# A fused cross-attention kernel: the mask moves from TensorE products to ScalarE copies into the banks of scores

## The chip, the cores and the metric

The kernel runs on one core of one Trainium2 chip. The metric is the device time of one execution in microseconds (us), from the first to the last instruction and what lies around them. Lower is better.

## The reference, cut to what matters

The input is 32 sequences of 64 tokens with 128 features, a context of the same shape, and a mask of 32 x 64 booleans that says for each sequence which keys are valid. Three attention layers follow one another, each with 16 heads of 64: self-attention with a causal mask, cross-attention and a feed-forward network (128, 512, 128), and a third attention with rotary positions.

```python
scores = jnp.einsum('bhqd,bhkd->bhqk', q, k)
if causal:
    scores = jnp.where(causal_mask[None, None], NEG_INF, scores)
if padding_mask is not None:
    scores = jnp.where(padding_mask[:, None, None, :], scores, NEG_INF)
attn = jax.nn.softmax(scores / math.sqrt(DK), axis=-1)
out = jnp.einsum('bhqk,bhkd->bhqd', attn, v)
```

After each layer comes a residual sum and a layer norm. The kernel adds -1e30 to a masked score instead of replacing it.

## The kernel before, in words

**Units.** A unit is two sequences (128 tokens) in one layer. There are 16 units a layer, N = 48 in all, and one loop over steps `u` from FIRST = -2 to N + 1 that every engine walks in its own program order; only semaphores tie the engines together. In step `u` the kernel computes scores and softmax of unit `u`, turns and weights the probabilities of unit `u - 1` and `u - 2`, and projects queries (even `u`) or keys (odd `u`) of a later pair of units.

**Banks.** PSUM has eight banks of 128 x 512 f32. Two hold scores (`ps_s`), two the weighted values (`ps_o`), and four (`ps_p`) form a ring for everything else. `fills(u)` (line 59) is the list of what TensorE puts into the ring in step `u`, in order: T (tokens turned), V0 and V1 (values), P0 and P1 (probabilities turned), Q0 to Q3 or K0 to K3 (queries or keys; Qa, Qb, Ka, Kb in the rotary layer), Y (output projection), FT, F1, F2 (feed-forward). A fill waits until the fill four places earlier has been emptied by its engine (line 418 ff.). So in an odd step K0 waits for the copy of V0 out of its bank, and K1 for that of V1; in an even step, where T comes first, Q0 waits for V0 and Q1 for V1.

**TensorE in a step** (lines 521 to 535): `scores(u)`, then `weight_values(u)` (line 400), then the fills. `scores` (line 370) waits until VectorE has read the scores of the unit before (`shifted`), then issues four products with a 64 x 64 identity (line 388) that write the mask of each sequence into the four quarters of the two score banks, 512 columns each with the 64 keys repeated over 8 heads. Then 64 products of one head each (line 395) add to them.

**ScalarE in a step** (lines 597 to 618): it copies the two `ps_o` banks out (line 568), then walks the fills it has to empty. Ahead of each of the first two of them that isn't T it puts one exponential (`exponentials`, line 571, over 128 x 512). The order in an odd step is: heads, heads, exp 0, copy V0, exp 1, copy V1, copy P0, copy P1, copies of K0, K2, K3. In an even step T stands ahead of exp 0. In a step with feed-forward the order is exp 0, V0, exp 1, FT, V1, P0, P1. VectorE empties K1 or Q1, and all of the rotary Qa to Kb.

**VectorE in a step** (`vector_order`, line 126): two maxima over the score banks (line 698), two subtractions from them (line 702, they release `shifted`), T or FT's low part, the sum of the exponentials (line 709, after exp 1), reciprocal, emptying, two scalings (line 721), emptying, and the layer norm's statistics.

**The mask table.** The SP queue loads `mask_u8` (line 326), all 16 x 2 x 64 bytes on each of 128 partitions. VectorE makes from it the bf16 table `mask` (lines 744 to 751) for units 0 to 3 in step -1 and for the rest in step 2, and `valid` (lines 753 to 761, a maximum over the keys) in steps 0, 3 and 5. Products of `eye` with itself into `ps_s[0]` (line 514, `keep_clock`) run in the first microseconds.

**Steps with extra work.** Steps 14, 15, 16 and 30, 31, 32 split the weights of the next layer on ScalarE and VectorE (`split_high`, `split_rest`). In steps 16 and 32 V0 and V1 stand at the end of the fills. Steps 21 to 35, odd, have the feed-forward. Steps 30 to 45 project with rotary tables; steps 46 and on project nothing.

Of the kernel before, what the change touches and what calls it, by code (L numbers as in the profile page):

```python
# [6 lines left out]
ALU = mybir.AluOpType  # L7
# [90 lines left out]
ALL_FILLS = [(u, n, j, who) for u in range(FIRST, END) for n, j, who in fills(u)]  # L98

SCORED = Tally(lambda u: [()] if attends(u) else [])  # L100
SHIFTED = Tally(lambda u: [(0,), (1,)] if attends(u) else [])
# [36 lines left out]
def build(nc, a, out):  # L138
    ctx = ExitStack()
    with ctx:  # L140
# [40 lines left out]

        mask_u8 = sb("mask_u8", [128, UNITS, 2, S], mybir.dt.uint8)
        mask = sb("mask", [128, 2, UNITS, 2, S], BF16)
        causal = sb("causal", [128, S], BF16)
# [68 lines left out]
        act_emptied = sem("act_emptied")  # L253
        dve_emptied = sem("dve_emptied")
        scored = sem("scored")
        shifted = sem("shifted")
# [24 lines left out]
        READY = 4  # L281
        FIRST_MASKED, FIRST_VALID, MASKED, VALID, OTHER_VALID = 2, 5, 7, 10, 13

# [32 lines left out]
        def _(sp):  # L316
# [8 lines left out]
            sp.dma_start(columns[:, :], a["columns"]).then_inc(first_loaded, 16)  # L325
            sp.dma_start(mask_u8[:, :, :, :], a["mask_BxS2_bf1"].rearrange("(u b) k -> u b k", b=2).partition_broadcast(128))\
              .then_inc(mask_loaded, 16)
            sp.dma_start(w_raw[2][:, :], weight(0, "v")).then_inc(w_loaded[2], 16)
# [33 lines left out]
        def _(pe):  # L362
# [7 lines left out]
            def scores(u):  # L370
                par, v, layer = u // 2 % 2, u % 2, u // UNITS

                if SHIFTED.before(u):
                    pe.wait_ge(shifted, SHIFTED.before(u))

# [7 lines left out]

                for h in range(2):
                    for b in range(2):
                        of = slice(64 * h, 64 * h + 64)
                        m = mask[of, 0 if layer == 0 else 1, u % UNITS, b:b + 1, :]
                        mm(ps_s[h ^ b][64 * b:64 * b + 64, :], eye_bf[of, of], m.broadcast_to([64, 8, S]),  # L388
                           start=True, stop=False, skip_group_check=True)
                for p in range(PAIRS):  # L390
# [122 lines left out]

            def keep_clock(n):

                for _ in range(n):
                    mm(ps_s[0][:, 0:128], eye[:, :], eye[:, :], start=True, stop=True)

            pe.wait_ge(setup_pool, EYES)
            keep_clock(2)  # L520
            for u in range(FIRST, END):
                if u in (0, READY):
                    pe.wait_ge(setup_dve, MASKED if u else FIRST_MASKED)
                if attends(u):
                    scores(u)
                if u == 2:
                    pe.wait_ge(bvwo_read, 2)
                if finishes(u):
                    weight_values(u)
                for at, (name, j, _) in enumerate(fills(u)):  # L530
                    fill(u, at, name, j)
                    if u == FIRST and name == "T":
                        keep_clock(4)
                if u == 1:
                    bias_of_values()

        @block.scalar
        def _(act):
# [32 lines left out]
            def exponentials(u, j):  # L571
                act.wait_ge(shifted, SHIFTED.at(u, j))
                p = probs[:, u % 2, j::2, :]
                nc.scalar.activation(p, p, ACT.Exp, scale=float(D) ** -0.5).then_inc(exped, 1)  # L574

            def split_high(u, after_input=False):
# [20 lines left out]
            for u in range(FIRST, END):  # L597
# [7 lines left out]
                for at, (name, j, who) in enumerate(fills(u)):  # L605
                    if "A" not in who:
                        continue
                    if waiting and name not in ("O", "T"):
                        exponentials(u, waiting.pop(0))
                    empty(u, at, name, j)  # L610
                    if name == "T":
                        if u == FIRST:
                            split_high(u)
                        split_high(u, after_input=True)
                        if u == -2:
                            act.wait_ge(first_loaded, 16)
# [4 lines left out]
        def _(dve):  # L621
# [122 lines left out]
            def masks(units, count):  # L744
                V.tensor_scalar(mask[:, 1, units, :, :], mask_u8[:, units, :, :], -NEG, NEG, ALU.mult, ALU.add)\
                 .then_inc(setup_dve, 1)
                dve.wait_ge(setup_dve, count - 1)
                n = units.stop - units.start
                V.tensor_tensor(mask[:, 0, units, :, :].rearrange("q u b k -> q (u b) k"),
                                mask[:, 1, units, :, :].rearrange("q u b k -> q (u b) k"),  # L750
                                causal[:, None, :].broadcast_to([128, 2 * n, S]), ALU.min).then_inc(setup_dve, 1)

            def keys_at_all(kind, units, masked, count):

                dve.wait_ge(setup_dve, masked)
                for b in range(2):
                    of = slice(64 * b, 64 * b + 64)
                    V.tensor_reduce(valid[of, kind, units], mask[of, kind, units, b, :], AX_X, ALU.max).then_inc(setup_dve, 1)
                dve.wait_ge(setup_dve, count - 1)
# [3 lines left out]
            def before_m1():  # L763
                dve.wait_ge(mask_loaded, 16)
                dve.wait_ge(setup_pool, CAUSAL)
# [212 lines left out]
```

## Time and profile before

| what | value |
|---|---|
| times of three runs | 607.12 us median, 605.61 to 608.26 |
| the profiled execution | 603.87 us, span 602.1 us |
| granted TensorE clock, mean | 0.99 |
| TensorE products, weight loads | 555.6 us (92%), 509.2 us (85%) |
| VectorE, ScalarE, GpSimd | 459.0 us (76%), 302.1 us (50%), 335.5 us (56%) |
| mask products (line 388) | 192, 19.7 us busy in all |
| exponentials (line 574) | 96, mean 638 ns |

Matmuls overlap each other, so a busy TensorE is not one at its peak; the spacing of starts says more than durations do. In the timeline a row of several instructions has the start of the first and the length of all of them. "idle before <-releaser" names how long the engine had stood still and what ended that.

### The profile page before, as it was taken

The page shows a single profiled execution, that of the slowest core. Times are in us where ns is not written, and L with a number is a line of the kernel's source. Part 1 is how long each engine was busy: PE and PEld are TensorE (multiplying, and loading weights), DVE is VectorE, ACT ScalarE, POOL GpSimd, SP SyncE. Part 2 cuts the span into 40 slices and gives each one's busy share as a digit, 9 for nine tenths or more (in the row PEclk, how much of TensorE's full clock was granted, in tenths as well). Part 3 has the DMA queues.
Part 4 walks back from the last instruction along what each step waited for, and adds up shares of the span by engine and source line. Part 5 has one row for each costly group of instructions (what it writes and reads, how often), then busy time and mean ns, then how long its engine had stood idle before and what let it go on. Part 6 is the DMA issues. An engine that isn't in the chain of part 4 may idle for free.

```text
span 602.1 us, 22151 instructions
## 1 busy us (share of the span) xinstructions
PE 555.6 (92%) x9632; PEld 509.2 (85%) x9632; DVE 459.0 (76%) x902; ACT 302.1 (50%) x647; POOL 335.5 (56%) x665
## 2 busy tenths in 40 slices
PE   6699999999998999999999988899999989999984
PEld 6588798989897988988989878789898979898874
DVE  4977877777777767677767798888888878888862
ACT  6365666575866666557565742242322424222252
POOL 1613535354436353648457496877676555465635
PEclk9979999999999999999999998999999999999999
DMA  8900000000111100000000000000000000000000
GB/s 244 282 2 3 3 2 2 2 4 2 37 37 37 38 4 2 3 2 3 2 3 3 2 3 1 1 3 2 7 7 7 7 10 7 7 7 7 5 12 14
DMA packets 10975, 12.44 MB, mean 21 GB/s; under 512 B 1024, under 2 KB 8704, under 8 KB 10880
## 3 DMA queue, kind: packets, MB, share of 16 engines
q1 hardware_dynamic: 10880, 11.04, 6.2%
q8 instruction: 76, 1.25, 0.9%
q14 instruction: 19, 0.16, 0.1%
HBM read 9.99 MB, written 1.05 MB: 18 GB/s over the span
## 4 chain that ended last, share of the span: by engine, by line
PE 60%; DVE 19%; ACT 8%; POOL 8%; issue 4%; DMA 1%; SPq 0%; POOLq 0%; ACTq 0%; DVEq 0%
PE ps_p L366 10%; PE ps_p L481 10%; PE ps_p L367 8%; PE ps_p L368 8%; PE ps_s L395 5%; PE ps_o L410 5%; PE ps_p L455 3%; ACT probs L574 3%; DVE top L698 3%; DVE probs L721 3%; PE ps_p L503 2%; ACT vv L549 2%; DVE rope_b L655 2%; ACT headsT L568 2%; PE ps_s L388 2%
## 5 line engine op out<-in xcount | busy, mean ns | idle before, releaser
L568 ACT ACTIVATE headsT<-ps_o 128x512 f32<-128x512 f32 x96 | 52.2, 596 | 206.9 <-PE ps_o L410 206.9
L481 PE MATMUL ps_p<-wo,headsT 128*128 128x128 f32 x768 | 94.1, 276 | 2.3 <-ACT headsT L568 1.3
L481 PEld LDWEIGHTS ps_p<-wo,headsT 128*128 128x128 f32 x768 | 89.7, 192 | 3.6 <-DVE rope_a L655 1.5
L709 DVE TENSOR_REDUCE total<-probs 128x16 f32<-128x1024 f32 x48 | 58.4, 1216 | 36.2 <-ACT probs L574 36.2
L698 DVE TENSOR_REDUCE top<-ps_s 128x8 f32<-128x512 f32 x96 | 61.7, 685 | 26.3 <-PE ps_s L395 26.1
L847 POOL TENSOR_TENSOR small<-mv,epsilon 128x1 f32<-128x1 f32 x48 | 17.9, 374 | 113.0 <-DVE mv L691 111.8
L721 DVE TENSOR_TENSOR probs<-probs,rinv 128x512 f32<-128x512 f32 x96 | 68.2, 713 | 0.0
L574 ACT ACTIVATE probs<-probs 128x512 f32<-128x512 f32 x96 | 61.2, 638 | 12.7 <-DVE probs L702 12.7
L366 PE MATMUL ps_p<-xT_hi,wq_hi 128*128 128x256 f32 x192 | 59.5, 310 | 5.9 <-DVE xT_lo L642 3.3
L455 PE MATMUL ps_p<-eye,probs 128*128 128x128 f32 x384 | 53.9, 275 | 9.7 <-ACT vv L549 2.9
L549 ACT ACTIVATE vv<-ps_p 128x512 f32<-128x512 f32 x96 | 57.5, 599 | 9.3 <-PE ps_p L450 9.1
L455 PEld LDWEIGHTS ps_p<-eye,probs 128*128 128x128 f32 x384 | 44.2, 140 | 20.8 <-issue 6.2
L702 DVE TENSOR_TENSOR probs<-ps_s,top 128x512 f32<-128x512 f32 x96 | 61.3, 680 | 0.0
L827 POOL TENSOR_TENSOR qT<-rope_a,rope_b 128x512 f32<-128x512 f32 x32 | 45.7, 1440 | 26.2 <-DVE rope_b L655 25.2
L395 PEld LDWEIGHTS ps_s<-kT,qT 64*64 64x64 f32 x3072 | 53.2, 135 | 3.3
L410 PE MATMUL ps_o<-probsT,vv 64*64 64x64 f32 x3072 | 53.8, 218 | 2.3 <-issue 2.3
L551 ACT ACTIVATE probsT<-ps_p 128x512 f32<-128x512 f32 x96 | 53.5, 618 | 1.7 <-PE ps_p L455 1.6
L367 PE MATMUL ps_p<-xT_lo,wq_hi 128*128 128x256 f32 x192 | 54.3, 283 | 0.0
L368 PE MATMUL ps_p<-xT_hi,wq_lo 128*128 128x256 f32 x192 | 54.1, 282 | 0.0
L557 ACT ACTIVATE qT<-ps_p,columns 128x256 f32<-128x256 f32 x96 | 39.0, 489 | 28.7 <-PE ps_p L368 28.6
L395 PE MATMUL ps_s<-kT,qT 64*64 64x64 f32 x3072 | 53.0, 218 | 0.0
L410 PEld LDWEIGHTS ps_o<-probsT,vv 64*64 64x64 f32 x3072 | 49.5, 135 | 2.8 <-issue 2.5
(144 smaller groups left out, 1480.3 us busy)
## 6 DMA issues: line engine op xcount, KB each, us to landing
out<-y_out SPq DMA_DIRECT2D x16, 64.0 KB, 1.5
X<-in_x SPq DMA_DIRECT2D x1, 768.0 KB, 8.0
across<-in_across SPq DMA_DIRECT2D x1, 704.0 KB, 10.4
wq_raw<-in_L_xattn_sa_wq SPq DMA_DIRECT2D x2, 256.0 KB, 3.1
wk_raw<-in_L_xattn_sa_wk SPq DMA_DIRECT2D x1, 512.0 KB, 5.1
wv_raw<-in_L_xattn_sa_wv SPq DMA_DIRECT2D x1, 512.0 KB, 7.7
wo<-in_L_xattn_sa_wo SPq DMA_DIRECT2D x1, 512.0 KB, 8.8
wo<-in_L_xattn_ca_wo SPq DMA_DIRECT2D x1, 512.0 KB, 10.1
```

Of the source, the lines that this page charges most:

```text
L366: mm(dst, w[0], x[0], start=True, stop=False)
L367: mm(dst, w[0], x[1], start=False, stop=False)
L368: return mm(dst, w[1], x[0], start=False, stop=True)
L395: last = mm(ps_s[h ^ b][64 * b:64 * b + 64, 64 * p:64 * p + 64], qT[of, par, p, t:t + S], kT[of, par, p, t:t + S], start=False, stop=True, ...
L410: last = mm(ps_o[b][64 * c:64 * c + 64, 64 * p:64 * p + 64], vv[of, w % 2, c, p, :], probsT[of, p // HALF, q:q + 64], start=True, stop=Tru ...
L455: last = nc.tensor.transpose(bank[:, 128 * pp:128 * pp + 128], probs[:, (u - 1) % 2, at_head:at_head + 2, :].rearrange("q h k -> q (h k)") ...
L481: last = mm(bank[:, 0:E], headsT[:, p, :, :].rearrange("r b q -> r (b q)"), wo[:, layer % 2, p, :], start=(p == 0), stop=(p == PAIRS - 1))
L549: ins = nc.scalar.activation(vv[:, u % 2, j, :, :].rearrange("k p d -> k (p d)"), bank[:, :], ACT.Copy)
L568: nc.scalar.activation(headsT[:, :, b, :], ps_o[b][:, :].rearrange("r (p q) -> r p q", q=S), ACT.Copy)\
L574: nc.scalar.activation(p, p, ACT.Exp, scale=float(D) ** -0.5).then_inc(exped, 1)
L698: V.tensor_reduce(top[:, j, :], score_heads(j), AX_X, ALU.max).then_inc(dve_step, 1)
L721: V.tensor_tensor(p, p, rinv[:, 8 * j:8 * j + 8, None].broadcast_to([128, 8, S]), ALU.mult)\
```

## The change

The mask products leave TensorE. ScalarE writes the masks: after exponential `j` of unit `u` it copies the mask of unit `u + 1` from SBUF into score bank `j`, and TensorE's score products add to what lies there. The table is now by query: partitions 0 to 63 hold the masks of the unit's first sequence, 64 to 127 those of the second, so it has half as many columns; it is loaded by two DMAs instead of one. `open_scores` takes the place of `keep_clock`: four products into each score bank at the start.

```diff
-        mask_u8 = sb("mask_u8", [128, UNITS, 2, S], mybir.dt.uint8)
-        mask = sb("mask", [128, 2, UNITS, 2, S], BF16)
+        mask_u8 = sb("mask_u8", [128, UNITS, S], mybir.dt.uint8)
+        mask = sb("mask", [128, 2, UNITS, S], BF16)
...
-            sp.dma_start(mask_u8[:, :, :, :], a["mask_BxS2_bf1"].rearrange("(u b) k -> u b k", b=2).partition_broadcast(128))\
-              .then_inc(mask_loaded, 16)
+            for b in range(2):
+                rows_of = a["mask_BxS2_bf1"].rearrange("(u b) k -> b u k", b=2)[b, :, :]
+                sp.dma_start(mask_u8[64 * b:64 * b + 64, :, :], rows_of.partition_broadcast(64)).then_inc(mask_loaded, 16)
...
             def scores(u):
...
-                if SHIFTED.before(u):
-                    pe.wait_ge(shifted, SHIFTED.before(u))
+                pe.wait_ge(masked, OPENED.at(u, 1))
...
-                for h in range(2):
-                    for b in range(2):
-                        of = slice(64 * h, 64 * h + 64)
-                        m = mask[of, 0 if layer == 0 else 1, u % UNITS, b:b + 1, :]
-                        mm(ps_s[h ^ b][64 * b:64 * b + 64, :], eye_bf[of, of], m.broadcast_to([64, 8, S]),
-                           start=True, stop=False, skip_group_check=True)
...
-            def keep_clock(n):
-
-                for _ in range(n):
-                    mm(ps_s[0][:, 0:128], eye[:, :], eye[:, :], start=True, stop=True)
+            def open_scores(j):
+
+
+                for k in range(4):
+                    last = mm(ps_s[j][:, 128 * k:128 * k + 128], eye[:, :], eye[:, :], start=(k == 0), stop=(k == 3),
+                              skip_group_check=True)
+                last.then_inc(opened, 1)
 
             pe.wait_ge(setup_pool, EYES)
-            keep_clock(2)
+            open_scores(0)
             for u in range(FIRST, END):
-                if u in (0, READY):
-                    pe.wait_ge(setup_dve, MASKED if u else FIRST_MASKED)
                 if attends(u):
                     scores(u)
...
                     if u == FIRST and name == "T":
-                        keep_clock(4)
+                        open_scores(1)
...
                 nc.scalar.activation(p, p, ACT.Exp, scale=float(D) ** -0.5).then_inc(exped, 1)
+                if attends(u + 1):
+                    put_masks(u + 1, j)
+
+            def put_masks(u, j):
+
+                if u == 0:
+                    act.wait_ge(opened, j + 1)
+                else:
+                    act.wait_ge(shifted, SHIFTED.at(u - 1, j))
+                if u in (0, READY):
+                    act.wait_ge(setup_dve, MASKED if u else FIRST_MASKED)
+                m = mask[:, u // UNITS and 1, u % UNITS, None, :].broadcast_to([128, PAIRS, S])
+                nc.scalar.activation(ps_s[j][:, :].rearrange("q (p k) -> q p k", k=S), m, ACT.Copy).then_inc(masked, 1)
...
                     empty(u, at, name, j)
+                    if (u, name, j) == (-1, "K", 0):
+                        for k in range(2):
+                            put_masks(0, k)
...
-                V.tensor_scalar(mask[:, 1, units, :, :], mask_u8[:, units, :, :], -NEG, NEG, ALU.mult, ALU.add)\
-                 .then_inc(setup_dve, 1)
+                V.tensor_scalar(mask[:, 1, units, :], mask_u8[:, units, :], -NEG, NEG, ALU.mult, ALU.add).then_inc(setup_dve, 1)
...
-                for b in range(2):
-                    of = slice(64 * b, 64 * b + 64)
-                    V.tensor_reduce(valid[of, kind, units], mask[of, kind, units, b, :], AX_X, ALU.max).then_inc(setup_dve, 1)
+                V.tensor_reduce(valid[:, kind, units], mask[:, kind, units, :], AX_X, ALU.max).then_inc(setup_dve, 1)
...
-                dve.wait_ge(mask_loaded, 16)
+                dve.wait_ge(mask_loaded, 32)
```
The constants FIRST_MASKED, FIRST_VALID, MASKED, VALID, OTHER_VALID go from 2, 5, 7, 10, 13 to 2, 4, 6, 8, 10, as `keys_at_all` has one reduction instead of two.

## Rows read from the trace of the kernel before

**Rows 1.** Groups of instructions, each form apart: the mask products of TensorE

```profile
L388 PE MATMUL ps_s<-mask,eye_bf 64*64 64x512 bf16 x192 | 19.7, 399 | 5.3 <-DVE kT L313 3.1 <-issue 2.1
```

**Rows 2.** Waits, TensorE's weight loads: total us, times, longest us

```profile
PEld ps_p L366 <- ACT vv L549: 17.5, 36, 2.5
```

**Rows 3.** Timeline of TensorE, 104 to 115 us: steps 8 (even) and 9 (odd)

```profile
104.75 0.39 PE L366 MATMUL ps_p<-xT_hi,wq_hi 128*128 128x256 f32 x1
...
108.87 0.41 PE L388 MATMUL ps_s<-mask,eye_bf 64*64 64x512 bf16 x4
109.11 1.10 PE L395 MATMUL ps_s<-kT,qT 64*64 64x64 f32 x64
...
113.38 0.38 PE L366 MATMUL ps_p<-xT_hi,wk_hi 128*128 128x256 f32 x1
...
114.39 0.39 PE L366 MATMUL ps_p<-xT_hi,wk_hi 128*128 128x256 f32 x1
```

**Rows 4.** Timeline of ScalarE over the same two steps

```profile
104.08 0.62 ACT L549 ACTIVATE vv<-ps_p 128x512 f32<-128x512 f32 x1
...
112.21 0.63 ACT L574 ACTIVATE probs<-probs 128x512 f32<-128x512 f32 x1
112.75 0.58 ACT L549 ACTIVATE vv<-ps_p 128x512 f32<-128x512 f32 x1
113.22 0.62 ACT L574 ACTIVATE probs<-probs 128x512 f32<-128x512 f32 x1
113.74 0.59 ACT L549 ACTIVATE vv<-ps_p 128x512 f32<-128x512 f32 x1
```

**Rows 5.** Timeline of VectorE, 110 to 115 us: step 9

```profile
110.29 1.29 DVE L698 TENSOR_REDUCE top<-ps_s 128x8 f32<-128x512 f32 x2 [1.33 <-PE ps_s L395]
111.50 1.28 DVE L702 TENSOR_TENSOR probs<-ps_s,top 128x512 f32<-128x512 f32 x2
```

**Rows 6.** Timeline of three engines, 259 to 261 us: a step with feed-forward

```profile
259.70 0.37 ACT L547 ACTIVATE x2T_hi<-ps_p 128x256 fp32r<-128x256 f32 x1
...
260.10 0.42 DVE L645 TENSOR_TENSOR x2T_lo<-ps_p,x2T_hi 128x256 fp32r<-128x256 f32 x1 [1.38 <-ACT x2T_hi L547]
...
260.63 0.35 PE L366 MATMUL ps_p<-cT_hi,wk_hi 128*128 128x256 f32 x1 [0.64 <-ACT vv L549]
```

**Rows 7.** Timeline of VectorE and TensorE, 510 to 519 us: step 41, odd and rotary

```profile
510.17 1.22 DVE L709 TENSOR_REDUCE total<-probs 128x16 f32<-128x1024 f32 x1 [1.11 <-ACT probs L574]
...
518.88 0.41 PE L388 MATMUL ps_s<-mask,eye_bf 64*64 64x512 bf16 x4 [0.63 <-DVE kT L313]
```

**Rows 8.** Timeline of the start: ScalarE and TensorE ahead of unit 0's scores

```profile
11.36 1.06 ACT L591 ACTIVATE wv_hi<-wv_raw 128x1024 fp32r<-128x1024 f32 x1 [0.82 <-DMA wv_raw<-in_L_xattn_sa_wv]
12.32 2.28 ACT L557 ACTIVATE kT<-ps_p,columns 128x256 f32<-128x256 f32 x6
...
14.70 0.41 PE L388 MATMUL ps_s<-mask,eye_bf 64*64 64x512 bf16 x4 [1.83 <-issue]
```

**Rows 9.** DMA view of 5.6 to 6.0 us (mostly 208-byte rows): packets and share

```profile
DMA packets 99, 0.06 MB, mean 139 GB/s; under 512 B 88, under 2 KB 88, under 8 KB 99
...
q1 hardware_dynamic: 99, 0.06, 54.7%
```

**Rows 10.** DMA view of 6.4 to 6.8 us (the mask's 2-KB rows)

```profile
DMA packets 26, 0.07 MB, mean 179 GB/s; under 512 B 1, under 2 KB 1, under 8 KB 26
...
q1 hardware_dynamic: 26, 0.07, 136.9%
```

**Rows 11.** Groups of instructions, each form apart: VectorE's maxima over the mask table

```profile
L758 DVE TENSOR_REDUCE valid<-mask 64x16 f32<-64x1024 bf16 x2 | 2.4, 1210 | 0.0
L758 DVE TENSOR_REDUCE valid<-mask 64x12 f32<-64x768 bf16 x2 | 1.9, 942 | 0.0
```

**Rows 12.** TensorE after a long stall; busy time in 30 to 37 us (after POOL the clock)

```profile
31.23 0.58 PE L366 MATMUL ps_p<-xT_hi,wk_hi 128*128 128x256 f32 x1 [2.22 <-ACT vv L549]
...
30.00:37.00 7.00, 5.77 (x27) 5.77 (x28) 5.14 (x10) 4.91 (x11) 1.25 (x1) 0.52 0.00 0
```

More of the change, by code:

```diff
@@ L98 @@
 ALL_FILLS = [(u, n, j, who) for u in range(FIRST, END) for n, j, who in fills(u)]
+OPENED = Tally(lambda u: [(0,), (1,)] if attends(u) else [])
 SCORED = Tally(lambda u: [()] if attends(u) else [])
@@ L254, in build @@
         dve_emptied = sem("dve_emptied")
+        opened = sem("opened")
+        masked = sem("masked")
         scored = sem("scored")
@@ L281, in build @@
         READY = 4
-        FIRST_MASKED, FIRST_VALID, MASKED, VALID, OTHER_VALID = 2, 5, 7, 10, 13
+        FIRST_MASKED, FIRST_VALID, MASKED, VALID, OTHER_VALID = 2, 4, 6, 8, 10
         def parts_ready(layer, n):
@@ L744, in masks @@
             def masks(units, count):
-                V.tensor_scalar(mask[:, 1, units, :, :], mask_u8[:, units, :, :], -NEG, NEG, ALU.mult, ALU.add)\
-                 .then_inc(setup_dve, 1)
+                V.tensor_scalar(mask[:, 1, units, :], mask_u8[:, units, :], -NEG, NEG, ALU.mult, ALU.add).then_inc(setup_dve, 1)
                 dve.wait_ge(setup_dve, count - 1)
                 n = units.stop - units.start
-                V.tensor_tensor(mask[:, 0, units, :, :].rearrange("q u b k -> q (u b) k"),
-                                mask[:, 1, units, :, :].rearrange("q u b k -> q (u b) k"),
-                                causal[:, None, :].broadcast_to([128, 2 * n, S]), ALU.min).then_inc(setup_dve, 1)
+                V.tensor_tensor(mask[:, 0, units, :], mask[:, 1, units, :], causal[:, None, :].broadcast_to([128, n, S]),
+                                ALU.min).then_inc(setup_dve, 1)
             def keys_at_all(kind, units, masked, count):
                 dve.wait_ge(setup_dve, masked)
-                for b in range(2):
-                    of = slice(64 * b, 64 * b + 64)
-                    V.tensor_reduce(valid[of, kind, units], mask[of, kind, units, b, :], AX_X, ALU.max).then_inc(setup_dve, 1)
+                V.tensor_reduce(valid[:, kind, units], mask[:, kind, units, :], AX_X, ALU.max).then_inc(setup_dve, 1)
                 dve.wait_ge(setup_dve, count - 1)
```

## The prediction

> **What bounds the kernel now.** I read the groups by form first, then the waits, then the timeline of one quiet pair of steps (8 and 9), where the order of every instruction can be seen. The mask products look cheap: 192 of them, but only 19.7 us busy in all, since the four of a unit run side by side [rows 1]. The waits say that TensorE's weight loads stood still 36 times for ScalarE's copy of values, 17.5 us in all [rows 2]. The timeline shows why. K0 starts at 113.38 and K1 at 114.39 [rows 3]; the copies of V0 and V1 out of the same banks end at 112.75 + 0.58 = 113.33 and 113.74 + 0.59 = 114.33 [rows 4]. TensorE starts 0.05 us after each. The even step is the same: Q1 starts at 104.75 [rows 3], V1's copy ends at 104.08 + 0.62 = 104.70 [rows 4]. So from the scores to the second projection a step is a chain: scores, two maxima and a subtraction on VectorE [rows 5], exp 0, V0's copy, exp 1, V1's copy, K1 or Q1. ScalarE's share of 50% doesn't matter there; its order does. After K1 TensorE runs on without a stop to the next scores.
>
> **The change, part by part.** A quiet step first.
>
> Mask products removed: the four start at 108.87 and the score products at 109.11 [rows 3]. That is 0.24 us a unit, at the head of the chain: VectorE's maximum waits for the scores' end [rows 5], so exp 0 comes 0.24 us earlier. In an even step the maximum is late for VectorE's own reasons, but there exp 0 stands behind heads and T on ScalarE, which follow TensorE and move up too.
>
> Mask copies added: ScalarE has one 128 x 512 copy more behind each exponential, ahead of V0's and V1's. No such write into a score bank is in the trace. What one takes on a full engine is the spacing of starts: 0.54 us (112.21 to 112.75) and 0.52 us (113.22 to 113.74) behind an exponential, which reads SBUF as the mask copy does, and 0.47 us (112.75 to 113.22) behind a copy out of PSUM [rows 4]. The bounds are 0.47 and 0.54; I take 0.52. V0 is then emptied 0.52 us later and V1 1.04 us. K0 starts 0.52 us later; it takes 0.72 us without stalls, so K1, held by V1, starts 1.04 us later. Both waits are already binding, so nothing absorbs it: what follows (P0 and P1 copied 1.04 us later) is needed 0.7 us and more after K1 and is no new wait. A quiet step grows by 1.04 - 0.24 = 0.80 us. ScalarE makes up for it in its idle time ahead of the next heads, but TensorE doesn't get it back.
>
> One rule of the Trainium skill bears on the price: ScalarE: Activation LUTs, section Step-by-step, says that PSUM is the lower-latency destination for an ACTIVATE. No run here has a ScalarE write into PSUM. By it each copy might take the lower bound, and the sum would come out some 3.5 us lower.
>
> With feed-forward, the order is exp 0, V0, exp 1, FT, V1. K0 needs FT's low part: ScalarE at 259.70, VectorE at 260.10 + 0.42 = 260.52, K0 at 260.63 [rows 6]. FT now stands behind both mask copies, so K0 starts 1.04 us later: again 0.80 us net.
>
> Steps where it is so: 1 to 13, 15, 17 to 29, 33 and 35, and the even ones from 34 to 44, whose projections TensorE bounds; 13 + 1 + 13 + 2 + 6 = 35 steps, 35 x 0.80 = 28.0 us.
>
> Odd rotary steps without feed-forward (37, 39, 41, 43, 45): VectorE works from the sum at 510.17 without a pause to the last key sum, for which TensorE waits 0.63 us at 518.88 [rows 7]. The sum waits for exp 1 alone, which has one mask copy ahead of it: 0.52 - 0.24 = 0.28 us, 5 x 0.28 = 1.4 us.
>
> Steps 14, 16, 30, 31, 32: splitting weights on VectorE holds the low parts longer than ScalarE is late, or V0 and V1 stand last. Only the removed products count: -5 x 0.24 = -1.2 us. Step 46 has no projection, but Y takes V0's bank: +0.3 us. Step 47 has no mask behind it: about 0.
>
> Start: the two mask copies of unit 0 stand on ScalarE between the copies of K0 and K2; that run goes from 12.32 to 14.60 and releases the scores at 14.70 [rows 8]. +1.04 - 0.24 = 0.8 us. The mask's load stands in the SP queue ahead of that of the V weights, and ScalarE waits for those at 11.36 [rows 8], so each us of the mask's load is a us of the start. Before, it is 128 packets of 2 KB, 8 on each DMA engine; 26 packets, nearly all such, took 136.9% of 16 engines in 0.4 us: 8.76 us / 26 = 337 ns each [rows 10], 2.7 us an engine. After, a partition's row is 16 pieces of 64 bytes from places 128 bytes apart, so 2048 packets, 128 an engine. The nearest packets are those of 208 bytes: 99 with 54.7% of 16 engines in 0.4 us are 35 ns each, and some 25 ns if the 11 large ones are taken out [rows 9]. 128 x 25 ns = 3.2 us, 0.5 us more than now; with the second issue I take +0.7 us. Bounds: -2.7 us (packets for nothing) and 128 x 337 ns - 2.7 = +40 us (each as dear as the mask's rows now). I keep near the small packets, but the same few bytes are read by 64 partitions, which may be what makes the 2-KB rows dear; so +8 us belongs in the range. The Trainium skill, DMA: Bandwidth & Descriptors, Specifications, speaks against this edit: below 512 bytes a transfer isn't at line rate and becomes a read-modify-write. It gives no price; with packets twice as dear as rows 9 show, the start would take 3 us more.
>
> Half the table on VectorE: the conversions in step 2 are hidden behind TensorE. The maxima over the table in steps 3 and 5 were late work ahead of the scores' maxima: 1.9 us and 2.4 us become half [rows 11], -0.95 - 1.2 = -2.15 us. The products that open the banks are covered by the wait for the first weights; if that cover were gone, two more products cost under 1 us.
>
> Sum: 28.0 + 1.4 - 1.2 + 0.3 + 0.8 + 0.7 - 2.15 = +27.9 us. Against the profiled execution's own 603.87 us that makes 631.7; that execution is 3.2 us below the median of the runs, 607.12. Against the median it is **635.0 us**, 4.6% slower, which I forecast.
>
> **The rivals.**
>
> 1. Faster: TensorE is the bound and ScalarE's slack swallows the copies. Then only removals count: 48 x 0.24 + 2.15 = -13.7 us, 593.4. For it: TensorE 92% busy, ScalarE 50%. It needs the copies to fall behind the copy of V1, or to take under 0.12 us each (two of them against 0.24). Against it: the 36 waits [rows 2] and the 0.05 us between copy and product at both places. 4%.
> 2. Partly hidden: K1's delay is won back within the step, because waits for later banks or for VectorE vanish, so that only exp 1's delay counts everywhere, as in step 41. 47 x 0.28 + 0.8 + 0.7 - 2.15 = +12.5 us, 619.6. For it: VectorE is 76% busy and shares the chain. Against it: TensorE has no later stop in steps 8 and 9. 9%.
> 3. A dear load: small packets at 80 to 337 ns. +7 to +40 us on top, 642 to 675. For it: the rows of one place [rows 10]. Against it: rows 9. 6%.
> 4. The clock: TensorE stood still for 2.22 us until 31.23, the last of several stops, and the granted clock was 0.52 over 30 to 37 us [rows 12], so that it ran mostly at 1.2 GHz instead of 2.4; 7 us did the work of 3.6. If the longer stalls bring three to five such stretches, 10 to 17 us are added: 645 to 652. Against it: the new stalls are about 1 us, and stalls of that length left the mean granted clock at 0.99 over the whole execution. 5%.
> 5. It doesn't do what it says, for instance ScalarE's writes wait for something else than `shifted`: nothing in the diff shows it, and the times would be those of 2 or 3.
>
> **How the numbers follow.** Forecast 76%, the rivals 4, 9, 6 and 5%. The forecast's own bounds are 625 (copies at 0.47 us, cheap packets, the profiled execution's level) and 644 (0.54 us, +8 us of load). The range takes in rival 2 and the near end of 3 and 4: 619 to 648. A measurement of this kernel tells about 0.5% (3 us) from no change. Faster by more than that: rival 1, 0.04. Within it: the low tail of rival 2, 0.03. Slower: 0.93.
>
> **What would show it.** In the profile after: mask copies of about 0.6 us, 96 of them, starting 0.5 us after each exponential; V1's copy 1.5 us behind V0's instead of 1.0; K1 or Q1 still 0.05 us after V1's copy; TensorE's waits for that copy longer by about 0.5 us each; a pair of quiet steps 1.6 us longer; scores of unit 0 at about 16.2 us. The forecast is wrong if the second projection starts well after V1's copy, if a pair of steps is no longer than before, or if the V weights land several us later.

## The result

| | before | after |
|---|---|---|
| median, us | 606.57 (605.61 to 608.26, 4 runs) | 628.75 (628.05 to 636.12, 4 runs) |
| profiled execution, us | 603.87 | 628.05 |
| its span, us | 602.1 | 626.3 |
| mean granted clock | 0.990 | 0.987 |

The changed kernel is slower: the ratio is 1.040, with a 95% interval of 1.036 to 1.044. By the medians it takes 22.2 us more, by the profiled executions 24.2 us; 27.9 us were forecast.

The page of the kernel after, parts 1 and 4 (busy time of each engine; the chain that ended last, by engine), and two of its groups of instructions (out <- in, busy us, mean ns):

```profile
PE 554.9 (89%) x9444; PEld 505.7 (81%) x9444; DVE 455.7 (73%) x899; ACT 350.9 (56%) x743; POOL 337.1 (54%) x665
...
PE 52%; ACT 30%; DVE 12%; issue 3%; POOL 2%; DMA 1%; SPq 1%; ACTq 0%; POOLq 0%; DVEq 0%
...
L392 PE MATMUL ps_s<-kT,qT 64*64 64x64 f32 x3072 | 56.1, 222 | 5.9 <-DVE kT L316 3.0
...
L585 ACT ACTIVATE ps_s<-mask 128x512 f32<-128x512 bf16 x96 | 57.7, 602 | 0.0
```

The waits of the kernel after, for the first instruction of a projection, held by the copy of values (total us, times, longest us):

```profile
PEld ps_p L370 <- ACT vv L547: 53.4, 73, 3.0
PE ps_p L370 <- ACT vv L547: 35.8, 61, 2.7
```

ScalarE is still busy for only 56% of the span, yet its share of the chain went from 8% to 30%. The wait of [rows 2] went from 17.5 us in 36 places to 53.4 us in 73. Where a wait of 36 became one of 73, K0 or Q0, behind V0's copy, has joined K1 or Q1.

The same quiet step 9 as in [rows 3], TensorE's timeline of the kernel after:

```profile
110.02 1.16 PE L392 MATMUL ps_s<-kT,qT 64*64 64x64 f32 x64
...
114.86 0.39 PE L370 MATMUL ps_p<-xT_hi,wk_hi 128*128 128x256 f32 x1 [0.28 <-ACT vv L547]
...
116.39 0.38 PE L370 MATMUL ps_p<-xT_hi,wk_hi 128*128 128x256 f32 x1 [0.55 <-ACT vv L547]
```

and ScalarE's, which answers to [rows 4]:

```profile
113.17 0.63 ACT L572 ACTIVATE probs<-probs 128x512 f32<-128x512 f32 x1
113.71 0.58 ACT L585 ACTIVATE ps_s<-mask 128x512 f32<-128x512 bf16 x1
114.23 0.58 ACT L547 ACTIVATE vv<-ps_p 128x512 f32<-128x512 f32 x1
114.71 0.62 ACT L572 ACTIVATE probs<-probs 128x512 f32<-128x512 f32 x1
115.23 0.59 ACT L585 ACTIVATE ps_s<-mask 128x512 f32<-128x512 bf16 x1
115.75 0.58 ACT L547 ACTIVATE vv<-ps_p 128x512 f32<-128x512 f32 x1
```

V0's copy ends at 114.23 + 0.58 = 114.81 and K0 starts at 114.86; V1's ends at 116.33 and K1 starts at 116.39. Each mask copy takes ScalarE 0.52 us (113.71 to 114.23, and 115.23 to 115.75), and each copy of values stands later by just that.

**Where the 24.2 us came.** The growth of every step is read from the start of each unit's first product into the score banks (a mask product before, a score product after). Those of units 0 and 47 are 565.04 us apart before and 588.76 after. Grouped as the prediction grouped them:

| | forecast, us | measured, us |
|---|---|---|
| ahead of unit 0's first product, and step 0 | +0.8 (copies) + 0.7 (load) | +0.46 (ahead) + 0.17 (step 0) |
| 27 quiet steps apart from the next two rows | 27 x 0.80 = 21.6 | +22.94 (0.85 on average) |
| steps 21, 23, 25, 27, 29 (odd, feed-forward) | 5 x 0.80 = 4.0 | +2.28 |
| steps 1, 3, 5 | 3 x 0.80 - 2.15 = +0.25 | -3.25 + 0.02 - 0.51 = -3.74 |
| odd rotary 37, 39, 41, 43, 45 | +1.4 | +1.74 |
| steps 14, 16, 30, 31, 32 | -1.2 | +1.44 |
| step 46 | +0.3 | -1.11 |
| sum | +27.9 | +24.18 |

Of the 27 quiet steps 24 grew by 0.84 to 1.01 us. Step 15 grew by 0.44, and steps 40 and 42 by -0.53 and +2.52, as a pause of TensorE moved from the one to the other (below).

### The profile page after: what moved, and what is told of

It is laid out like the page before. It is cut to its first block, busy times and chain, and to the rows that moved or that the text cites. A ratio compares the mean times of both kernels' runs of the same rounds, so it can differ in the third digit from the quotient of the medians.

```text
span 626.3 us, 21872 instructions
## 1 busy us (share of the span) xinstructions
PE 554.9 (89%) x9444; PEld 505.7 (81%) x9444; DVE 455.7 (73%) x899; ACT 350.9 (56%) x743; POOL 337.1 (54%) x665
## 4 chain that ended last, share of the span: by engine, by line
PE 52%; ACT 30%; DVE 12%; issue 3%; POOL 2%; DMA 1%; SPq 1%; ACTq 0%; POOLq 0%; DVEq 0%
PE ps_p L478 11%; PE ps_p L370 9%; PE ps_s L392 8%; ACT probs L572 8%; ACT headsT L566 7%; PE ps_p L371 7%; PE ps_p L372 7%; ACT vv L547 7%; PE ps_o L407 7%; ACT ps_s L585 7%; PE ps_p L500 2%; DVE rope_a L669 2%; DVE probs L735 2%; DVE total L723 2%; DVE rope_b L669 1%
## 5 line engine op out<-in xcount | busy, mean ns | idle before, releaser
L735 DVE TENSOR_TENSOR probs<-probs,rinv 128x512 f32<-128x512 f32 x96 | 65.4, 685 | 0.0
L392 PE MATMUL ps_s<-kT,qT 64*64 64x64 f32 x3072 | 56.1, 222 | 5.9 <-DVE kT L316 3.0
L392 PEld LDWEIGHTS ps_s<-kT,qT 64*64 64x64 f32 x3072 | 49.6, 135 | 12.8 <-issue 7.8
L585 ACT ACTIVATE ps_s<-mask 128x512 f32<-128x512 bf16 x96 | 57.7, 602 | 0.0
L370 PEld LDWEIGHTS ps_p<-xT_hi,wq_hi 128*128 128x128 f32 x192 | 36.7, 191 | 22.0 <-ACT vv L547 16.1
```

The lines of the kernel that those rows point to most:

```text
L370: mm(dst, w[0], x[0], start=True, stop=False)
L392: last = mm(ps_s[h ^ b][64 * b:64 * b + 64, 64 * p:64 * p + 64], qT[of, par, p, t:t + S], kT[of, par, p, t:t + S], start=False, stop=True, ...
L585: nc.scalar.activation(ps_s[j][:, :].rearrange("q (p k) -> q p k", k=S), m, ACT.Copy).then_inc(masked, 1)
L735: V.tensor_tensor(p, p, rinv[:, 8 * j:8 * j + 8, None].broadcast_to([128, 8, S]), ALU.mult)\
```

## The experiments

Theory: the price is the two mask copies' place in ScalarE's sequence, ahead of V0's and V1's copies, 0.52 us each; TensorE's removed products give back some 0.2 us. Rivals: the work itself costs it wherever it stands; the load in small packets costs or gains; TensorE's score products are slower for adding to ScalarE's data. The comparisons below are each with the kernel before, run beside it.

**e1_late_gap.** Both mask copies of a step in ScalarE's idle time: behind the copy of Q0 in an even step, K3 in an odd one, F1 with feed-forward, P1 in the rotary layer.

```diff
-                if attends(u + 1):
-                    put_masks(u + 1, j)
...
+                    if attends(u) and attends(u + 1) and (name, j) == mask_place(u):
+                        for k in LATE:
+                            put_masks(u + 1, k)
```

> The changed kernel, but ScalarE writes both masks later in the step: behind the copy of Q0 (even steps), of K3 (odd steps), of F1's first half (steps with feed-forward), or of P1 (rotary steps). Theory A (the cost is the place, two writes ahead of V1's copy; work on ScalarE as such is free): V0's and V1's copies are back where they were, about 8 us below the kernel before (near 598 us): 3 us from the start, 0.2 us a step from the removed products, less 0.2 to 0.4 us in the ten odd steps where ScalarE has no gap left. Theory B (the added work or TensorE's adding to a written bank costs in itself): 606 us or more.

Measured: 594.83 us (593.6 to 596.53), ratio 0.982 (0.978 to 0.985). The same 96 copies, and the kernel is faster than both. ScalarE's timeline of e1, step 9:

```profile
106.86 0.63 ACT L583 ACTIVATE probs<-probs 128x512 f32<-128x512 f32 x1
107.40 0.58 ACT L558 ACTIVATE vv<-ps_p 128x512 f32<-128x512 f32 x1
107.87 0.62 ACT L583 ACTIVATE probs<-probs 128x512 f32<-128x512 f32 x1
108.39 0.59 ACT L558 ACTIVATE vv<-ps_p 128x512 f32<-128x512 f32 x1
108.87 1.09 ACT L560 ACTIVATE probsT<-ps_p 128x512 f32<-128x512 f32 x2
109.82 2.51 ACT L566 ACTIVATE kT<-ps_p,columns 128x256 f32<-128x256 f32 x6
112.21 1.13 ACT L594 ACTIVATE ps_s<-mask 128x512 f32<-128x512 bf16 x2
```

and TensorE's:

```profile
109.04 0.39 PE L381 MATMUL ps_p<-xT_hi,wk_hi 128*128 128x256 f32 x1
...
113.40 0.81 PE L403 MATMUL ps_s<-kT,qT 64*64 64x64 f32 x40 [0.16 <-ACT ps_s L594]
```

Exponentials and copies of values stand as close as in [rows 4], and the wait for the copy of values is back at 15.3 us in 36 places. Even steps are 0.17 to 0.20 us shorter than before, odd ones 0.04 longer, since there the next scores wait 0.16 us for the mask copy that ends at 113.34. That is what was expected. The profiled execution, 596.43 us, is 7.4 us below that of the kernel before, where about 8 were expected; most of the other executions were shorter (the median is 10 us below that of the kernel before), and no trace shows what differed in them.

**e2_late_p1.** The same with both copies behind P1's in every step but step 0.

```diff
+def mask_place(u):
+    return ("P", 1) if u else ("Q", 0)
```

> Both masks behind the copy of P1 in every step. Theory A: nearly as fast as the version in the gaps, about 600 to 603 us, as K0's copy is late for Y's bank by 0.4 us in odd steps. Theory B: as above, 606 us or more.

Measured: 597.76 us (596.13 to 598.52), ratio 0.986 (0.983 to 0.989). Even steps are 0.18 to 0.20 us shorter than before, but odd ones grow by 0.41, as there the masks stand ahead of the copies of K. The time is 2 us under the 600 to 603 expected. The place within ScalarE's later work is worth 3 us, against e1; the place ahead of V0's and V1's copies costs 31 us, against e2.

**e3_bank1_late.** Only bank 1's mask behind P1; bank 0's stays behind exponential 0.

```diff
-LATE = (0, 1)
+LATE = (1,)
```

> Only the mask of bank 1 behind P1's copy, that of bank 0 still ahead of V0's. Theory A: V1's copy is late by one write (0.52 us) instead of two, so a quiet step grows by 0.52 - 0.19 = 0.33 us instead of 0.85: about 615 us, some 13 us below the changed kernel. Theory B: within 3 us of the changed kernel.

Measured: 612.0 us (611.27 to 613.56), ratio 1.009 (1.006 to 1.013). A quiet step grows by 0.33 to 0.41 us. Two early copies, one, none: +0.85, +0.33 and -0.18 us for an even step, so a copy costs 0.52 us whether it is the first or the second, and nothing when it is late. That holds for even steps. An odd step grows by 0.41 in e3 and in e2 alike: there the copies behind P1 already cost 0.6 us (-0.19 without any, in e5), and one early copy adds nothing to it. The whole came out 3 us under the 615 expected.

**e4_write_beside.** The kernel before with the change's mask copies added at the change's places; the mask products stay, wait for the copies (`masked`, in place of `shifted`) and overwrite them.

```diff
+                if attends(u + 1):
...
+                    m = mask[:, (u + 1) // UNITS and 1, (u + 1) % UNITS, 0:1, :].broadcast_to([128, PAIRS, S])
+                    nc.scalar.activation(ps_s[j][:, :].rearrange("q (p k) -> q p k", k=S), m, ACT.Copy).then_inc(masked, 1)
```

> The kernel before with its mask products kept, and ScalarE's writes added at the changed kernel's places (TensorE then overwrites them). This is the added cost alone, without the removal and without the start's changes. Theory A: quiet steps grow by 1.04 us, in all 33 to 37 us: about 641 us, slower than the changed kernel by 12. If the start's changes gave nothing (rival): about 637 us.

Measured: 649.07 us (647.11 to 650.4), ratio 1.071 (1.066 to 1.075): +44 us by the medians. A quiet step grows by 1.04 us, 2 x 0.52 to the hundredth, the 27 of them by 28.1 us. TensorE's timeline of e4, step 10, shows the same two stops as the kernel after:

```profile
123.12 0.39 PE L367 MATMUL ps_p<-xT_hi,wk_hi 128*128 128x256 f32 x1 [0.27 <-ACT vv L550]
...
124.65 0.39 PE L367 MATMUL ps_p<-xT_hi,wk_hi 128*128 128x256 f32 x1 [0.55 <-ACT vv L550]
```

Most of the 8 us above the 641 expected lie in a few steps that grew by 1.5 to 2.7 us (5, 21, 29, 30, 40), some 6 us more in all than their like. Busy time by windows of e4 (the number before the last two is the granted clock; the columns are the window, its length, and PE, PEld, DVE, ACT, POOL busy):

```profile
80.00:84.00 4.00, 3.84 (x23) 3.57 (x22) 2.59 (x6) 2.92 (x8) 0.00 (x0) 0.66 0.00 0
84.00:88.00 4.00, 4.00 (x150) 3.74 (x148) 2.27 (x6) 0.82 (x3) 1.26 (x4) 1.00 0.01 4
...
255.00:260.00 5.00, 3.84 (x19) 3.48 (x18) 2.43 (x5) 3.28 (x8) 0.00 (x0) 0.68 0.01 3
```

Each of the two stands behind a wait of TensorE for the copy of values that the longer step made longer:

```profile
78.91 0.38 PE L367 MATMUL ps_p<-xT_hi,wk_hi 128*128 128x256 f32 x1 [1.86 <-ACT vv L550]
...
256.55 0.36 PE L367 MATMUL ps_p<-cT_hi,wk_hi 128*128 128x256 f32 x1 [1.16 <-ACT vv L550]
```

In windows of 10 us the mean clock is under 0.95 in nine of e4's, against three of the kernel before and five of the kernel after. TensorE ran part of such a stretch at 1.2 instead of 2.4 GHz, and each stretch costs 1 to 1.7 us. So the forecast's fourth rival exists, and the stops ahead of these two stretches were of 1.9 and 1.2 us. A stop of that length doesn't settle it: the same one of 1.16 us ends at 284.3, 310.3 and 336.3 in e4, and in the five odd steps with feed-forward of the changed kernel, with the clock at full behind it, while in e6 (below) two of these five are followed by a slow stretch. In the changed kernel, whose steps are 0.2 us shorter, such a stretch lengthened step 30 against the kernel before; those in step 1 are told below.

**e5_no_products.** The kernel before without the mask products, nothing in their place: the masks aren't applied. The price of the removal alone.

```diff
-                        mm(ps_s[h ^ b][64 * b:64 * b + 64, :], eye_bf[of, of], m.broadcast_to([64, 8, S]),
-                           start=True, stop=False, skip_group_check=True)
...
-                                      start=False, stop=True, skip_group_check=True)
+                                      start=True, stop=True, skip_group_check=True)
```

> The kernel before without its mask products: no mask is applied at all, so this is the removal alone. If a unit's four products cost what the start of the scores moves (0.24 us): 11.5 us less, 595 us. If they cost what quiet steps of the changed kernel show (1.04 - 0.85 = 0.19 us): 9 us less, 597.5 us. If VectorE or GpSimd absorb half of it: 601 us or more.

Measured: 599.37 us (598.43 to 602.36), ratio 0.989 (0.985 to 0.994): -6.7 us by the medians, between the 9 us expected at 0.19 a step and the 5 or less of the last theory. A quiet step is 0.18 to 0.20 us shorter, not 0.24. TensorE's timeline of e5:

```profile
108.63 1.16 PE L389 MATMUL ps_s<-kT,qT 64*64 64x64 f32 x64
```

The score products now take 1.16 us instead of the 1.10 of [rows 3], whether ScalarE's data lies in the bank (after) or not (e5). So adding to ScalarE's data costs nothing. Perhaps the mask products used to cover the start of the first ones; that was not tried. In the steps with feed-forward a pair of steps gains nothing (-0.19 and +0.18): the pair isn't bound by the chain of [rows 3] there. And 1.04 - 0.19 = 0.85 us is the changed kernel's quiet step: the two halves add up.

**e6_row_load.** The change with the old load of the mask (one DMA, whole rows of 2 KB on all partitions); the table is halved when VectorE converts it.

```diff
-            for b in range(2):
-                rows_of = a["mask_BxS2_bf1"].rearrange("(u b) k -> b u k", b=2)[b, :, :]
-                sp.dma_start(mask_u8[64 * b:64 * b + 64, :, :], rows_of.partition_broadcast(64)).then_inc(mask_loaded, 16)
+            sp.dma_start(mask_u8[:, :, :, :], a["mask_BxS2_bf1"].rearrange("(u b) k -> u b k", b=2).partition_broadcast(128))\
+              .then_inc(mask_loaded, 16)
```

> The changed kernel with the mask loaded as before: one DMA of whole 2048-byte rows, VectorE taking its half of each. If the 2048 small packets were cheaper than the 128 large ones (the V weights landed 0.6 us earlier): the V weights land at 11.3 us again and the scores of unit 0 start 0.5 us later, total within 1 us of the changed kernel (629 to 630 us). If the small packets cost more than the large ones: up to 1 us faster than the changed kernel.

Measured: 630.47 us (628.81 to 637.1), ratio 1.042 (1.033 to 1.050), against the change's 1.040: no difference that can be told in the time. The timeline can: the split of the V weights on ScalarE starts at 11.24 us, against 10.78 after and 11.36 before, and the first scores at 15.61, against 15.16 after. So the 64-byte rows bring the V weights sooner, by about 0.5 us. All traces agree: the V weights have landed by 10.58 to 11.06 us in the six runs with 64-byte rows, by 11.21 to 11.98 in the six with rows of 2 KB. The first scores don't show it by themselves: they start between 15.16 and 15.87 us in the six with 64-byte rows, and e6's 15.61 lies among them. ScalarE's timeline after, then e6's:

```profile
10.78 1.06 ACT L602 ACTIVATE wv_hi<-wv_raw 128x1024 fp32r<-128x1024 f32 x1 [0.30 <-DMA wv_raw<-in_L_xattn_sa_wv]
```

```profile
11.24 1.06 ACT L601 ACTIVATE wv_hi<-wv_raw 128x1024 fp32r<-128x1024 f32 x1
```

**What made step 1 shorter.** After the change, step 1 is 3.25 us shorter than before, and 3.3 to 4.9 us in e1, e2, e3 and e6, but not in e4 (+0.72) or e5 (-0.65). VectorE's timeline of the kernel before, at unit 0's probabilities:

```profile
18.84 0.85 DVE L758 TENSOR_REDUCE valid<-mask 64x4 f32<-64x256 bf16 x2
19.73 1.75 DVE L760 TENSOR_SCALAR valid<-valid 128x4 f32<-128x4 f32 x1
21.51 1.22 DVE L709 TENSOR_REDUCE total<-probs 128x16 f32<-128x1024 f32 x1
...
24.35 3.88 DVE L721 TENSOR_TENSOR probs<-probs,rinv 128x512 f32<-128x512 f32 x2
```

GpSimd's beside it:

```profile
19.55 1.90 POOL L891 TENSOR_TENSOR rope_a<-wo,columns 128x1024 f32<-128x1024 f32 x1
21.53 2.63 POOL L896 TENSOR_TENSOR rope_a<-rope_a 128x512 f32<-128x512 f32 x3
24.12 1.90 POOL L891 TENSOR_TENSOR rope_b<-wo,columns 128x1024 f32<-128x1024 f32 x1
```

A comparison of 128 x 4 numbers took 1.75 us, and ended at 21.48, just as GpSimd's product ended at 21.45. The two scalings took 3.88 us, where all 96 average 713 ns each. The kernel after, VectorE's timeline:

```profile
19.42 0.41 DVE L768 TENSOR_REDUCE valid<-mask 128x4 f32<-128x256 bf16 x1
19.86 0.17 DVE L770 TENSOR_SCALAR valid<-valid 128x4 f32<-128x4 f32 x1
20.86 1.22 DVE L723 TENSOR_REDUCE total<-probs 128x16 f32<-128x1024 f32 x1 [0.83 <-ACT probs L572]
...
24.14 1.55 DVE L735 TENSOR_TENSOR probs<-probs,rinv 128x512 f32<-128x512 f32 x2
```

The half table's maxima take 0.41 us instead of 0.85, the comparison slips in ahead of GpSimd's product (which starts at 20.16), and the scalings meet the short additions rather than the long product. Runs e7 to e10 test that.

There is a second cause. Step 1 ends with K's 24 products, and in the kernel before the granted clock is 0.52 around them [rows 12]. Cut at the start of K0, with K's products measured to the start of the next product:

| us | before | after | e1 | e2 | e5 | e7 | e9 |
|---|---|---|---|---|---|---|---|
| unit 1's first product to K0 | 9.13 | 6.47 | 5.42 | 5.41 | 9.14 | 5.41 | 6.54 |
| K's 24 products | 5.29 | 4.71 | 4.71 | 3.26 | 4.66 | 3.26 | 3.27 |

The first row is VectorE's part: 3.72 us less without early mask copies (e1, e2 and e7), of which the two copies of the changed kernel take 1.06 back. The second is the clock's: 3.26 us at full clock, up to 5.29 where it is down. So of the 3.25 us after the change 2.66 are the first and 0.58 the second, and the 0.65 us of e5 are the clock alone.

**e7_maxima_early.** The kernel before with the table's maxima in VectorE's idle time ahead of step 0's first maximum.

```diff
             def maximum(u, j):
+                if (u, j) == (0, 0):
+                    keys_at_all(0, slice(0, READY), FIRST_MASKED, FIRST_VALID)
...
             def sums(u):
-                if u == 0:
-                    keys_at_all(0, slice(0, READY), FIRST_MASKED, FIRST_VALID)
```

> The kernel before, with the maxima of the mask table (two reductions and the comparison, 0.85 and 1.75 us between 18.84 and 21.48) moved from between step 0's subtractions and its sum to ahead of step 0's first maximum, where VectorE idled 2.43 us. Nothing is left out. Theory A: step 1 of the changed kernel was 3.3 us shorter because VectorE's sequence at step 0 was shorter, and because its scalings then fell beside another of GpSimd's folding products (1.55 us for the two instead of 3.88). Then here the sum starts near 19.8 instead of 21.51, the scores of step 2 start at 34 to 36 us instead of 37.69, and the time is 602.5 to 605 against about 606.3. Theory B: the gain of that step came from the written masks or from TensorE's clock; then the time is within 1 us of the kernel before.

Measured: 602.17 us (600.2 to 606.82), ratio 0.994 (0.992 to 0.997). The sum starts at 20.41 and the scalings take 2.33 us. Unit 2's mask products start at 32.62 instead of 37.69, earlier than the 34 to 36 expected: the clock is at full over K's products, which is 2.03 us of the 5.07. Step 2 gives 2.82 us back, as unit 2's maxima now stand behind the conversion of the rest of the table (to 35.03 us), and the clock is down from 35.7 to 39.1; 2.25 us stay.

**e9_fold_held.** The kernel before with GpSimd's second folding held until step 0's scalings are done.

```diff
                 for layer in range(2):
+                    if layer:
+                        pool.wait_ge(normed, NORMED.at(0, 1))
```

> The kernel before, with GpSimd's second folding (the product from 24.12 and three additions to 29.35) held back until VectorE has done step 0's scalings. Nothing is left out. Theory A: an operation of VectorE that starts beside a folding product of GpSimd takes as long as that product still runs; then the two scalings take 1.3 us instead of 3.88, the scores of step 2 start 2 to 2.6 us earlier (35.1 to 35.7), the fold ends near 31 and its reader at 38 doesn't wait for it; time 603.5 to 604.5 against about 606.3. Theory B: the scalings are slow for another reason (their operands, their place in the start); then they stay near 3.9 us and the time doesn't fall.

Measured: 603.42 us (601.36 to 605.06), ratio 0.995 (0.993 to 0.997). VectorE's timeline of e9, then GpSimd's:

```profile
24.70 1.28 DVE L721 TENSOR_TENSOR probs<-probs,rinv 128x512 f32<-128x512 f32 x2
25.90 1.28 DVE L698 TENSOR_REDUCE top<-ps_s 128x8 f32<-128x512 f32 x2
```

```profile
26.06 1.90 POOL L893 TENSOR_TENSOR rope_b<-wo,columns 128x1024 f32<-128x1024 f32 x1 [1.55 <-DVE probs L721]
```

With the product out of the way the same two scalings take 1.28 us instead of 3.88. That is theory A of the expectation, to the size of it. The maxima from 25.90 on, which read PSUM, keep their 1.28 us beside the product; so does the sum, which reads SBUF (1.22 us from 20.86 in the kernel after, beside the product that runs from 20.16 to 22.05). The Trainium skill, SBUF — State Buffer, section SBUF: two separate sides, says that VectorE, in those of its instructions that need it, and GpSimd hold a shared pair of ports by turns, each for a whole instruction; the trace of the kernel before agrees, with the comparison that lasted until GpSimd's product was over (21.48 and 21.45).

Unit 2's mask products start at 33.39, though, 1.7 us ahead of the 35.1 to 35.7 expected. The expectation counted the scalings (2.6 us) and not the clock, which doesn't fall in the start of e9: K0 and the clock over 30 to 37 us, where [rows 12] have 31.23, 0.58 and 0.52:

```profile
28.98 0.39 PE L366 MATMUL ps_p<-xT_hi,wk_hi 128*128 128x256 f32 x1 [2.22 <-ACT vv L549]
...
30.00:37.00 7.00, 5.15 (x154) 4.80 (x154) 6.90 (x13) 3.21 (x8) 3.18 (x6) 1.00 0.01 2
```

The stop ahead of K0 is 2.22 us in both. That is 2.0 us more at unit 2, of which step 2 gives 1.55 back. How much of the 2.5 us between the medians belongs to either isn't shown; the length of the scalings is.

**e8_late_gap_early** and **e10_gap_fold_held.** e1 with each of these two edits.

> The kernel e1_late_gap (both masks written in ScalarE's gaps) with the maxima of the table moved ahead of step 0's first maximum as well. Theory A: in e1 the sum of step 0 waited little for them (it started at 20.75), so at most 0.5 us is left, unless the scalings (2.28 us for two) miss the folding products: 593.5 to 595.5, against 594.8 of e1. Theory B, in which VectorE's order at step 0 doesn't matter: 594.8, the same number, so this run alone doesn't decide; its timeline does.

Measured: 595.02 us (592.92 to 595.38), ratio 0.981 (0.979 to 0.984).

> The kernel e1_late_gap with GpSimd's second folding held until step 0's scalings are done, as in e9. If what each was worth adds up (-11.2 and -2.5 us), the time is 592 to 593 against about 606. But in e1 the scalings already took only 2.28 us for two, not 3.88, so at most 1.0 us is left there: 593.8. If e1's start already holds all that e9 gained, it is 594.8, e1's own.

Measured: 595.45 us (594.24 to 595.92), ratio 0.983 (0.981 to 0.985). Neither adds anything that can be told to e1's 594.83. In the profiled executions unit 47's scores start 1 us earlier than in e1 both times, after 1.5 us gained in step 1. But K0 stands 5.41 and 5.42 us behind unit 1's scores there, as in e1; the 1.5 us are the clock's (K's products take 3.27 us instead of 4.71), and neither edit can be credited with them. In e10 the scalings took 2.28 us as in e1, though the second folding was held: the first one still lay beside them. So what e7 and e9 gain on VectorE, e1 already has.

## Why the prediction was right

**The mechanism** was the one forecast, and the place of both waits was right: V0's and V1's copies each release a projection after 0.05 us, in the kernel after as before.

**The copies.** 0.52 us each, taken between 0.47 and 0.54, measured 0.52 in the timeline and 1.04 for two in e4's steps. They take 602 ns from start to end where the exponentials take 636, but the next copy starts no sooner for it, so the lower bound is not what they cost. The Trainium skill, ScalarE: Activation LUTs, Step-by-step, calls PSUM the lower-latency destination; the time from start to end agrees, the spacing of 0.52 us doesn't.

**The removed products.** 0.24 us forecast, 0.19 measured (e5), as the score products grew by 0.05. Over 27 quiet steps that is 27 x 0.05 = 1.3 us more than forecast.

**The sum is closer than its terms.** Its misses are -8.0 us (steps 1, 3 and 5, feed-forward, step 46, the start) and +4.3 us (the split steps, the quiet steps, the odd rotary ones), and they partly cancel. The misses of step 46 and of step 30, the larger part of that of the split steps, are a pause and a clock stretch that the sum didn't hold; that they pull in opposite directions is luck, not mechanism. The median came out 6.2 us under the 635.0: 3.7 us are the sum, the rest is that the forecast stood on the median of the kernel before and the changed kernel's profiled execution was its fastest.

**Feed-forward.** The step that failed: "again 0.80 us net" holds in the even steps, not in the odd ones, which grew by 0.77 once and by 0.35 to 0.40 in the rest (forecast 4.0 us for five, measured 2.28). Before, VectorE waited there for GpSimd's residual, and exponential 0 for VectorE. The timeline of VectorE, then of ScalarE, at step 23 of the kernel before:

```profile
254.92 0.29 DVE L675 TENSOR_TENSOR z<-ps_p,res 128x128 f32<-128x128 f32 x1 [2.04 <-POOL res L842]
...
258.16 0.63 ACT L574 ACTIVATE probs<-probs 128x512 f32<-128x512 f32 x1 [0.39 <-DVE probs L702]
```

The same two of the kernel after:

```profile
265.18 0.29 DVE L689 TENSOR_TENSOR z<-ps_p,res 128x128 f32<-128x128 f32 x1 [1.44 <-POOL res L852]
...
268.52 0.63 ACT L572 ACTIVATE probs<-probs 128x512 f32<-128x512 f32 x1
```

The wait of VectorE went from 2.04 to 1.44 us and that of exponential 0 from 0.39 to nothing. The slack absorbs about 0.47 us of such a step, in e4 as well (0.55 to 0.59 for 1.04, where the clock stays up), and it swallows the gain of e5. This is read from the rows; no run took GpSimd's residual away. The prediction had looked at FT in these steps, not at what held exponential 0.

**The table.** The maxima of steps 3 and 5 were priced well: 0.83 and 1.36 us off those steps (0.02 and -0.51 for 0.85), 2.2 us against 2.15. The maxima of step 0 were not priced at all; [rows 11] hold only the two later groups. Steps 1, 3 and 5 together came out 4.0 us under the forecast, all of it in step 1 (-3.25 for +0.80): the largest error of the sum. Of that step's 4.0 us 0.6 are the clock; the rest is VectorE's part, which e7 shows in full (5.41 us to K0, as in e1 and e2) and e9 for the scalings. The prediction took VectorE's durations as fixed, but in the start they depend on what GpSimd runs beside it.

**The load.** Forecast +0.7 us, between -2.7 and +40; measured -0.6 us at the V weights (10.78 after, 11.36 before). The DMA view of the kernel after, 6.8 to 7.2 us:

```profile
DMA packets 513, 0.03 MB, mean 86 GB/s; under 512 B 513, under 2 KB 513, under 8 KB 513
...
q1 hardware_dynamic: 513, 0.03, 87.7%
```

0.877 x 16 x 0.4 us / 513 = 10.9 ns a packet, not the 25 taken from [rows 9]; 128 of them are 1.4 us of an engine, where the rows of 2 KB took 2.7. The third rival is out. The Trainium skill, DMA: Bandwidth & Descriptors, Specifications, which speaks against short rows, is right on the rate (86 GB/s, against 179 in [rows 10]); no trace shows the read-modify-write that it names. Half the bytes took half the time all the same.

**Clock and pauses.** Steps 14, 16, 30, 31 and 32 were to lose 1.2 us and grew by 1.44: nothing in 14 and 16, and +1.48 in step 30. Before, the clock fell in step 31 and not in step 30, though TensorE stopped for 2.71 us at the same place of step 30; after, it fell in both. TensorE's timeline of the kernel after, in step 30:

```profile
364.05 1.09 PE L452 MATMUL ps_p<-eye,probs 128*128 128x128 f32 x4 [2.88 <-ACT probsT L549]
```

In the other direction, pauses of 1.1 to 1.4 us within the products of weights and values moved: before they were in steps 40 and 46, after in step 42. The profile names no cause ("issue"), and none was tried; together they make the changed kernel some 1.1 us shorter, the -1.11 of step 46 among it.

**The odd rotary steps** grew by 0.35 each (0.28 forecast): 0.52 less 0.19 is 0.33, so only the size of the removed products was off.

Rival 1, ScalarE's idle time swallowing the copies, is what e1 does: 594.8 measured for its 593.4. That the two are so close is chance, as 3.4 us of e1's gain lie in step 1, which the rival didn't count. It named its own condition, that the copies fall behind V1's, and the change didn't meet it. Rival 2 would have had every step grow by 0.28.

## What to carry to other kernels

An engine's busy share says nothing of what one more instruction on it costs. What counts is what stands behind it in its queue: here 0.52 us of ScalarE's time cost 0.52 us ahead of a copy that TensorE waits for, and nothing in an even step once that copy was out. Moving work to an idle engine pays when it is put where the engine idles: the same edit is 4.0% slower in one place and 1.8% faster in another (594.8 us, the fastest kernel of this study, level with e8 and e10). And a cheap instruction on VectorE can take the length of GpSimd's neighbour; look at the two timelines side by side before taking its duration as its own. When a stretch gets shorter, look at the granted clock there too before crediting the edit.

## What the runs showed of the hardware

- VectorE and GpSimd: two scalings of 128 x 512 numbers took 3.88 us beside a product of GpSimd, 2.28 to 2.34 or 1.55 at other offsets, and 1.28 with that product held back. A comparison of 128 x 4 took 1.75 us instead of 0.17.
- Packets of 64 bytes, read by 64 partitions each from the same few bytes, took 10.9 ns of a DMA engine each; rows of 2 KB read by 128 partitions took 337 ns each [rows 10].
- ScalarE's copy from SBUF into PSUM occupies it for 0.52 us, as an exponential from SBUF to SBUF does, at 602 against 636 ns from start to end.
- TensorE's granted clock averaged 0.66 over some 4 us after stops of 1.2 and 1.9 us in e4, and stayed at full after three more stops of 1.2 us; such a stretch cost 1 to 1.7 us (step 5 of e4 grew by 2.02 instead of 1.04, step 21 by 2.66). After the same stop of 2.22 us in step 1, K's 24 products took 5.29 us in the kernel before and 3.27 us in e9. Which stops bring it was not settled.
